# Splitting the gated activations before they are transposed, and transposing them by transfers from SyncE, in the expert stage of an early-fusion mixture-of-experts kernel

## The chip, the cores and the metric

The kernel runs on one core of one Trainium2 chip. The metric is the device time of one execution in microseconds. Five engines work side by side, each through its own instruction list in the order in which the program gives it: TensorE (PE in the profile, its weight loads PEld), VectorE (DVE), ScalarE (ACT), GpSimd (POOL) and SyncE (SP, which here only issues transfers). They meet at semaphores. Transfers run on 16 DMA engines that all queues share.

## The reference

```python
h = tokens(x)                             # 64 images -> 36 patches each, projected to 256, plus a class token
h = concatenate([h, txt], axis=1)         # 69 tokens x 64 = 4416 tokens of 256 values
h = h + attention(layernorm(h))
y = layernorm(h)
logits = y @ router                       # 8 experts, top 2 for each token
w13_out = ragged_dot(x_sort, moe_w13, group_sizes)      # 256 -> 1024, each expert its own weights
gate, up = split(w13_out, [512], axis=-1)
hidden = silu(gate) * up
out_dispatch = ragged_dot(hidden, moe_w2, group_sizes)  # 512 -> 256
h = h + zeros.at[token_ids_sort].add(out_dispatch * w_sort)
```

All is fp32. The change touches only what stands between `hidden` and `out_dispatch`, and the order around it.

## The kernel before

The program has two parts. `front()` does the patches, the attention, the router and the sorting of tokens to experts, and leaves three things: the normalised tokens with their weights for the experts in DRAM (`xn_rows`, 264 floats a row), the list `token_of` that says which 128 tokens make up each of 76 tiles, and `expert_of`, the expert of each tile. Some of the last tiles are padding, whose rows are all spare. It also fills `store_behind`, a number for each tile that says how far the scatters of the other parity must have come before its own scatter may go: for a tile whose expert differs from that of the tile before, and for every padding tile, it asks for the tile just before to have landed.

`experts()` then takes the 76 tiles one after the other (`N = TILES_MOE`). Each product is made of three fp16 products, since weights and activations are each split into a high and a low fp16 part (`terms`: hi by hi, hi by lo, lo by hi). For tile n:

- POOL gathers the tile's rows into `xg` (a piece of `wc`) by an indirect transfer; two buffers.
- PE transposes the 128x256 tile into bank 5 (two transposes by the identity); ACT copies it as fp16 to `x_hi`, DVE takes the difference as `x_lo`.
- PE makes the gate and the up product, 12 matmuls of 512 columns into `quad`; ACT takes the silu of the gate, DVE multiplies it with up into `hid`, fp32, 128 tokens by 512.
- PE transposes `hid` in four pieces of 128x128 into bank 4 (L1394); ACT copies that to `hid_hi` (L1307), DVE takes the difference as `hid_lo` (L1331).
- PE makes the second product, 12 matmuls of 256 columns, into bank 6 or 7 (L1424, through the helper at L1375); DVE scales it by the token's weight into `y` (L1354).
- POOL scatters `y` onto the output with addition, an indirect transfer (L1293). It waits for the scatter two tiles before, and for the one just before as far as `store_behind` asks.

The order on each engine is written out by hand in `step(t)`. On PE it is: transposes of hid(t-1), gate and up of t, transposes of x(t+1), second product of t-1. SP has nothing to do in this stage. Every intermediate has two buffers, chosen by the tile's parity. Below, step t starts with the first gate product of tile t.

## Time and profile before

| | |
|---|---|
| time, median of 3 runs | 825.34 us (822.24 to 830.76) |
| the profiled execution's own time | 829.55 us |
| its span in the trace | 827.4 us |
| mean granted clock of TensorE | 0.93 of full speed |
| expert stage in the trace, first transpose of a tile to the span's end | 462.3 to 827.4 us |
| busy share of the span: PE, DVE, POOL, ACT | 88%, 67%, 53%, 51% |
| DMA engines' mean busy share from 480 to 803 us | 0.38, at 60 GB/s |

The span is one profiled execution, times in it count from its start. A matmul's record is longer than the time until the next one starts, since matmuls are pipelined; the distance of starts is the rate. "issue" is time in which an engine waited for nothing that the profile shows. In rows of the kernel before, `bank<-idt,hid` is the transpose of the gated activations, `quad` the gate and up products, and `bank<-idt,wc` the transpose of a gathered tile.

### The profile page before, as it was taken

To read this page: it belongs to the slowest core of one execution; us is meant where nothing else is said; L and a number is where in the kernel's file an instruction comes from. 1 tells how busy PE (TensorE), PEld (TensorE's weight loads), DVE (VectorE), ACT (ScalarE), POOL (GpSimd) and SP (SyncE) were. 2 spreads that over 40 slices of the span, in tenths; PEclk is the share of its full clock that TensorE was granted. 3 is DMA by queue.
4 is the path that set the end of the run, shared out by engine and by line. 5 is a ranking of instruction groups with operands and counts; after the bars stand their busy time and mean duration, and the time that the engine had idled before them with its cause. 6 is when DMAs were issued, how large, how long until landed. Compare 5 with 4: busy or idle time off the path is not lost. (4 is left out here: it accounts for less than half of the span.)

```text
span 827.4 us, 27945 instructions
## 1 busy us (share of the span) xinstructions
PE 724.2 (88%) x9928; PEld 511.9 (62%) x9928; DVE 552.7 (67%) x1163; ACT 418.2 (51%) x951; POOL 435.6 (53%) x602
## 2 busy tenths in 40 slices
PE   6756989998999999989923599999999999999993
PEld 5634667776677776666722266666666666666662
DVE  6975888887888888787668455555555555555552
ACT  1233666677787777787637233333333333333330
POOL 5752554565766565553351255656555555555552
PEclk9985999999999999999655699999999999999997
DMA  8675576555454655454200034333333334343332
GB/s 286 210 240 177 152 244 190 152 163 153 138 163 147 174 159 153 125 169 123 82 25 7 27 54 66 54 64 57 62 59 60 60 59 65 55 66 54 64 55 24
DMA packets 64874, 91.81 MB, mean 111 GB/s; under 512 B 13176, under 2 KB 45704, under 8 KB 64679
## 3 DMA queue, kind: packets, MB, share of 16 engines
q1 hardware_dynamic: 49655, 66.81, 26.7%
q0 software_dynamic: 15088, 23.21, 16.8%
q8 instruction: 87, 1.43, 0.7%
q14 instruction: 44, 0.36, 0.1%
HBM read 58.95 MB, written 24.10 MB: 100 GB/s over the span
## 5 line engine op out<-in xcount | busy, mean ns | idle before, releaser
L1293 POOL DMA_INDIRECT out<-y,token_of x76 | 120.6, 1587 | 133.4 <-DVE own L1361 118.5
L1339 DVE SCALAR_TENSOR_TENSOR hid<-quad,up_scale,silu 128x512 f32<-128x512 f32 x76 | 57.0, 751 | 100.8 <-PE quad L1375 100.8
L1375 PE MATMUL quad<-w_hi,x_hi 128*128 x304 | 116.2, 382 | 1.2 <-DVE x_lo L1346 1.1
L1375 PE MATMUL quad<-w_lo,x_hi 128*128 x304 | 116.2, 382 | 0.0
L1375 PE MATMUL quad<-w_hi,x_lo 128*128 x304 | 116.2, 382 | 0.0
L652 DVE TENSOR_REDUCE nm_src<-quad 69x16 f32<-69x1104 f32 x64 | 83.0, 1297 | 35.4 <-PE quad L1055 35.2
L1307 ACT ACTIVATE hid_hi<-bank 128x512 f16<-128x512 f32 x76 | 45.4, 597 | 103.9 <-PE bank L1394 103.9
L919 ACT ACTIVATE probs<-quad 69x1104 f32<-69x1104 f32 x64 | 69.7, 1089 | 50.5 <-PE quad L1138 50.5
L1280 POOL DMA_INDIRECT wc<-xn_rows,token_of x74 | 73.4, 992 | 33.9 <-issue 21.9
L1375 PE MATMUL bank<-w_hi,hid_hi 128*128 x304 | 82.9, 273 | 1.6 <-ACT hid_hi L1307 1.6
L1375 PE MATMUL bank<-w_lo,hid_hi 128*128 x304 | 82.9, 273 | 0.0
L1375 PE MATMUL bank<-w_hi,hid_lo 128*128 x304 | 82.9, 273 | 0.0
L1313 ACT ACTIVATE silu<-quad,unscale 128x512 f32<-128x512 f32 x76 | 52.2, 687 | 54.8 <-PE quad L1375 54.8
L427 POOL TENSOR_SCALAR ve<-mv 128x1 f32<-128x1 f32 (+1 forms) x106 | 35.0, 330 | 63.8 <-DVE mv L715 35.6
L1331 DVE TENSOR_TENSOR hid_lo<-bank,hid_hi 128x512 f16<-128x512 f32 x76 | 52.6, 692 | 23.7 <-issue 19.1
L429 POOL TENSOR_TENSOR rs<-ve,eps_pow 128x1 f32<-128x1 f32 (+1 forms) x106 | 63.0, 595 | 8.8
L1319 ACT ACTIVATE x_hi<-bank 128x256 f16<-128x256 f32 x76 | 29.2, 384 | 74.2 <-PE bank L1415 74.2
L447 POOL TENSOR_TENSOR h<-hb,att 128x256 f32<-128x256 f32 (+1 forms) x35 | 34.4, 982 | 53.3 <-issue 27.2
L1354 DVE TENSOR_SCALAR y<-bank,weight 128x256 f32<-128x256 f32 x76 | 36.7, 483 | 35.3 <-PE bank L1375 35.3
L455 POOL TENSOR_TENSOR qk<-rot 128x256 f32<-128x256 f32 (+1 forms) x35 | 33.2, 949 | 48.1 <-DVE rot L697 47.9
L1134 PE MATMUL quad<-qT,kE 32*69 32x69 f32 x1024 | 45.9, 250 | 9.4 <-DVE nm_src L652 9.3
L1375 PEld LDWEIGHTS quad<-w_hi,x_lo 128*128 128x128 f16 x304 | 30.0, 99 | 36.2 <-issue 0.8
(230 smaller groups left out, 1866.0 us busy)
## 6 DMA issues: line engine op xcount, KB each, us to landing
w_lo<-in_experts_w SPq DMA_DIRECT2D x24, 512.0 KB, 5.9
w_raw<-in_experts_w SPq DMA_DIRECT2D x48, 256.0 KB, 4.9
xt<-in_patches SPq DMA_DIRECT2D x18, 384.0 KB, 5.7
h<-h_rows SPq DMA_DIRECT2D x34, 128.0 KB, 5.3
hb<-h_rows SPq DMA_DIRECT2D x34, 128.0 KB, 5.7
out<-h SPq DMA_DIRECT2D x34, 128.0 KB, 4.6
xn_rows<-xn SPq DMA_DIRECT2D x34, 128.0 KB, 4.6
vb<-v SPq DMA_DIRECT2D x30, 138.0 KB
```

Of the source, the lines that this page charges most:

```text
L429: nc.gpsimd.tensor_tensor(rs, ve, eps_pow[0:rs.shape[0], :], ALU.pow).then_inc(signal, 1)
L652: nc.vector.tensor_reduce(nm_src[b % 2][:, :].rearrange("p (g j) -> p g j", g=4)[:, :, 0:4], quad[0:SEQ, :, 0:4 * SEQ].rearrange("p g (j k ...
L919: nc.scalar.activation(probs[b % 2][:, :, :], quad[0:SEQ, :, 0:4 * SEQ], ACT.Exp, scale=HEAD_DIM ** -0.5).then_inc(s["probs_ready"], 1)
L1134: nc.tensor.matmul(quad[0:SEQ, g, j * SEQ:(j + 1) * SEQ], (kE, kO)[odd][band, c, at:at + SEQ], qT[band, c, at:at + SEQ], start=True, stop= ...
L1280: nc.gpsimd.indirect_dma_start(xg[q], None, xn_rows, bass.IndirectOffsetOnAxis(token_of[:, n:n + 1], 0)).then_inc(gathered[q], 16)
L1293: nc.gpsimd.indirect_dma_start(out, bass.IndirectOffsetOnAxis(token_of[:, n:n + 1], 0), y[q][:, :], None, compute_op=ALU.add).then_inc(add ...
L1307: nc.scalar.activation(hid_hi[q][:, :, :].rearrange("p c n -> p (c n)"), b4[:, :], ACT.Copy).then_inc(s["hid_hi_ready"], 1)
L1313: nc.scalar.activation(silu[q][:, :], quad[:, 2 * q, :], ACT.Silu, scale=unscale[:, 1:2]).then_inc(s["silu_ready"], 1)
L1331: nc.vector.tensor_tensor(hid_lo[q][:, :, :].rearrange("p c n -> p (c n)"), b4[:, :], hid_hi[q][:, :, :].rearrange("p c n -> p (c n)"), AL ...
L1339: nc.vector.scalar_tensor_tensor(out=hid[q][:, :], in0=quad[:, 2 * q + 1, :], scalar=up_scale[:, :], in1=silu[q][:, :], op0=ALU.mult, op1= ...
L1354: nc.vector.tensor_scalar(y[q][:, :], (b6, b7)[q][:, 0:DIM], weight[q][:, :], None, ALU.mult).then_inc(s["y_ready"], 1)
L1375: last = nc.tensor.matmul(dst, x[:, k, :], w[:, bass.ds(col + k * (2 * width if width == HIDDEN else width), width)], start=(k == 0 and m ...
```

## The change

The gated activations are now split first and transposed afterwards. ACT writes the fp16 high part of `hid` into half 0 of `hid_parts` (128 tokens x 2 x 512), DVE the low part into half 1, both from SBUF. SyncE then transposes the whole 128x1024 fp16 tile, eight blocks of 128x128, by one transfer into `hidT`, of which there are two. The second product of tile n moves from step n+1 to step n+2, and the scaling and the scatter with it. The scale factors `weight` get four buffers, the gathers three (`DEPTH`), and the first three gathers are issued by the front part. SyncE waits for both halves, and from tile 2 on for the second product of tile n-2, which frees the buffer that it writes. ACT and DVE wait, before they overwrite a half of `hid_parts`, for the transfer of tile n-2.

```diff
+DEPTH = 3
-        gathered = [sem(f"gathered{i}") for i in range(2)]
+        gathered = [sem(f"gathered{i}") for i in range(DEPTH)]
...
                     def _(pool):
                         def step(t):
-                            n, q, half, on, has = part(t + 2)
-                            if on and has(-2):
-                                pool.wait_ge(s["x_turned"], n - 1)
+                            n, q, half, on, has = part(t + DEPTH)
+                            if on and has(-DEPTH):
+                                pool.wait_ge(s["x_turned"], n - DEPTH + 1)
...
-                            n, q, half, on, has = part(t - 1)
+                            n, q, half, on, has = part(t - 2)
...
+                    @block.sync
+                    def _(sp):
+                        for n in range(N):
+                            q, half = n % 2, n // 2
+                            sp.wait_ge(s["hid_hi_ready"], n + 1)
+                            sp.wait_ge(s["hid_lo_ready"], n + 1)
+                            if n >= 2:
+                                sp.wait_ge(s["y_mm"], n - 1)
+                            sp.dma_start_transpose(hidT[q][:, :, :], hid_parts[q][:, :, :].rearrange("p a n -> p (a n)")).then_inc(hid_turned[q], 16)
...
                     def _(act):
-                            n, q, half, on, has = part(t - 1)
-                            if on:
-                                act.wait_ge(s["hid_turned"], n + 1)
-                                nc.scalar.activation(hid_hi[q][:, :, :].rearrange("p c n -> p (c n)"), b4[:, :], ACT.Copy).then_inc(s["hid_hi_ready"], 1)
...
+                            n, q, half, on, has = part(t)
+                            if on:
+                                act.wait_ge(s["hid_ready"], n + 1)
+                                if has(-2):
+                                    act.wait_ge(hid_turned[q], 16 * half)
+                                nc.scalar.activation(hid_parts[q][:, 0, :], hid[q][:, :], ACT.Copy).then_inc(s["hid_hi_ready"], 1)
...
                     def _(dve):
-                                nc.vector.tensor_tensor(hid_lo[q][:, :, :].rearrange("p c n -> p (c n)"), b4[:, :],
-                                                        hid_hi[q][:, :, :].rearrange("p c n -> p (c n)"), ALU.subtract).then_inc(s["hid_lo_ready"], 1)
...
+                            n, q, half, on, has = part(t)
+                            if on:
+                                dve.wait_ge(s["hid_hi_ready"], n + 1)
+                                if has(-2):
+                                    dve.wait_ge(hid_turned[q], 16 * half)
+                                nc.vector.tensor_tensor(hid_parts[q][:, 1, :], hid[q][:, :], hid_parts[q][:, 0, :], ALU.subtract).then_inc(s["hid_lo_ready"], 1)
+                            n, q, half, on, has = part(t - 2)
...
                     def _(pe):
-                            n, q, half, on, has = part(t - 1)
-                            if on:
-                                pe.wait_ge(s["hid_ready"], n + 1)
-                                if has(-1):
-                                    pe.wait_ge(s["hid_lo_ready"], n)
-                                for k in range(KH):
-                                    last = nc.tensor.transpose(b4[:, k * P:(k + 1) * P], hid[q][:, k * P:(k + 1) * P], idt[:, :])
-                                last.then_inc(s["hid_turned"], 1)
...
-                            n, q, half, on, has = part(t - 1)
+                            n, q, half, on, has = part(t - 2)
                             if on:
-                                pe.wait_ge(s["hid_hi_ready"], n + 1)
-                                pe.wait_ge(s["hid_lo_ready"], n + 1)
+                                pe.wait_ge(hid_turned[q], 16 * (half + 1))
```

On TensorE, between the second product of one tile (bank 6) and the gate product of the next, the list of before reads:

```order
L1375 MATMUL bank6<-w_lo,hid_hi0 128x256
L1375 MATMUL bank6<-w_hi,hid_lo0 128x256
L1394 MATMUL bank4<-idt,hid1 128x128 x4
L1375 ISA
L1375 MATMUL quad<-w_hi,x_hi0 128x512
```

and the changed one, where `hidT` takes the place of `hid_hi` and `hid_lo`:

```order
L1387 MATMUL bank7<-w_lo,hidT1 128x256
L1387 MATMUL bank7<-w_hi,hidT1 128x256
L1387 ISA
L1387 MATMUL quad<-w_hi,x_hi0 128x512
```

The four transposes are gone and nothing else stands in their place. Ahead of the gate product of an even tile (`x_hi0`) stood the second product of an even tile, two tiles back (`hid_hi0`); now that of an odd one stands there, three tiles back (`hidT1`).

On VectorE, one step in the middle of the stage, with the semaphores that each instruction waits for; before:

```order
L1331 TENSOR_TENSOR hid_lo1<-bank4,hid_hi1 128x512 [waits d_y_mm,d_hid_hi_ready]
L1339 SCALAR_TENSOR_TENSOR hid0<-quad,up_scale,silu0 128x512 [waits d_hid_turned,d_silu_ready,d_up_mm]
L1346 TENSOR_TENSOR x_lo1<-bank5,x_hi1 128x256 [waits d_up_mm,d_x_hi_ready]
L1354 TENSOR_SCALAR y1<-bank7,weight1 128x256 [waits d_added1,d_weight_ready,d_y_mm]
L1361 TENSOR_TENSOR own<-wc,is_expert 128x8 [waits d_weight_ready,gathered1]
```

and after:

```order
L1345 SCALAR_TENSOR_TENSOR hid0<-quad,up_scale,silu0 128x512 [waits d_hid_hi_ready,d_hid_lo_ready,d_silu_ready,d_up_mm]
L1352 TENSOR_TENSOR x_lo1<-bank5,x_hi1 128x256 [waits d_up_mm,d_x_hi_ready]
L1359 TENSOR_TENSOR hid_parts0<-hid0,hid_parts0 128x512 [waits d_hid_turned0,d_hid_hi_ready]
L1366 TENSOR_SCALAR y0<-bank6,weight2 128x256 [waits d_added0,d_weight_ready,d_y_mm]
L1373 TENSOR_TENSOR own<-wc,is_expert 128x8 [waits d_weight_ready,gathered2]
```

The low part is now taken of the tile of the same step (`hid0`, written two rows above it), behind `x_lo` and ahead of `y`, and it waits for a transfer's semaphore; the order of `hid` and `x_lo` is as it was.

On SyncE the stage was empty; now its list holds 76 rows like this one:

```order
L1310 DMA_TRANSPOSE hidT1<-hid_parts1 128x8x128 [waits d_y_mm,d_hid_lo_ready,d_hid_hi_ready]
```

SyncE has no other transfer in this stage, so a wait of it holds back only the transposes behind it.

## Rows read from the trace of the kernel before

**Rows 1.** Stretches: length, busy of PE, PEld, DVE, ACT, POOL; PEclk, DMA share, GB/s.

```profile
462.00:470.00 8.00, 6.41 (x16) 2.47 (x16) 1.23 (x4) 2.50 (x4) 0.94 (x1) 0.51 0.07 19
480.06:803.00 322.94, 322.94 (x2128) 215.00 (x2126) 176.56 (x426) 118.48 (x213) 183.27 (x142) 1.00 0.38 60
```

**Rows 2.** The chain that ended last, 598 to 606 us: start, length, engine, line.

```profile
598.65 2.59 PE quad L1375 x12
601.46 1.31 PE bank L1375 x12
602.77 0.44 PE bank L1394 x4
603.21 2.59 PE quad L1375 x12
```

**Rows 3.** By line and shape, 500 to 800 us: busy us, mean ns

```profile
L1394 PE MATMUL bank<-idt,hid 128*128 128x128 f32 x264 | 39.6, 273 | 0.0
L1331 DVE TENSOR_TENSOR hid_lo<-bank,hid_hi 128x512 f16<-128x512 f32 x66 | 45.6, 692 | 20.0 <-issue 17.8 <-ACT hid_hi L1307 2.2
L1307 ACT ACTIVATE hid_hi<-bank 128x512 f16<-128x512 f32 x66 | 39.4, 597 | 89.9 <-PE bank L1394 89.9
```

**Rows 4.** Timeline, one step around 601 us: start, length, engine, line, operation, [idle].

```profile
601.28 0.75 DVE L1339 SCALAR_TENSOR_TENSOR hid<-quad,up_scale,silu 128x512 f32<-128x512 f32 x1 [1.27 <-PE quad L1375]
601.29 0.27 PE L1375 MATMUL bank<-w_hi,hid_hi 128*128 x1
601.95 0.41 DVE L1346 TENSOR_TENSOR x_lo<-bank,x_hi 128x256 f16<-128x256 f32 x1
602.61 0.60 PE L1394 MATMUL bank<-idt,hid 128*128 128x128 f32 x4
602.81 0.48 DVE L1354 TENSOR_SCALAR y<-bank,weight 128x256 f32<-128x256 f32 x1 [0.45 <-PE bank L1375]
603.04 0.38 PE L1375 MATMUL quad<-w_hi,x_hi 128*128 x1
603.57 1.59 POOL L1293 DMA_INDIRECT out<-y,token_of  x1 [1.67 <-DVE own L1361]
```

**Rows 5.** DMA queues and us to landing, whole span, then 500 to 800 us.

```profile
q1 hardware_dynamic: 49655, 66.81, 26.7%
w_raw<-in_experts_w SPq DMA_DIRECT2D x48, 256.0 KB, 4.9
...
q0 software_dynamic: 12672, 17.58, 37.5%
out<-y,token_of POOLq DMA_INDIRECT x67, 3.9
```

**Rows 6.** Timeline of the stage's start, from the last gathers of the front part.

```profile
457.67 0.97 POOL L535 DMA_INDIRECT wc<-xn_rows,token_of  x1 [0.30 <-issue]
...
462.29 0.68 PE L1415 MATMUL bank<-idt,wc 128*128 128x128 f32 x2 [9.64 <-PEq L292]
470.27 0.42 DVE L1346 TENSOR_TENSOR x_lo<-bank,x_hi 128x256 f16<-128x256 f32 x1
470.94 0.39 PE L1375 MATMUL quad<-w_hi,x_hi 128*128 x1
474.41 0.41 DVE L1346 TENSOR_TENSOR x_lo<-bank,x_hi 128x256 f16<-128x256 f32 x1
475.50 0.38 PE L1375 MATMUL quad<-w_hi,x_hi 128*128 x1
```

**Rows 7.** Timeline of the stage's end: last tile's gate product, three of the scatters.

```profile
803.99 1.59 POOL L1293 DMA_INDIRECT out<-y,token_of  x1 [1.67 <-DVE y L1354]
...
808.02 0.38 PE L1375 MATMUL quad<-w_hi,x_hi 128*128 x1
...
809.44 1.57 POOL L1293 DMA_INDIRECT out<-y,token_of  x1 [3.86 <-DMA out<-y,token_of]
...
818.40 1.55 POOL L1293 DMA_INDIRECT out<-y,token_of  x1 [2.90 <-DMA out<-y,token_of]
```

More of the change, by code:

```diff
@@ L533, in _ @@
                             pool.wait_ge(xn_stored[par], 16 * len(range(par, G, 2)))
-                        for n in range(2):
+                        for n in range(DEPTH):
                             nc.gpsimd.indirect_dma_start(xg[n], None, xn_rows, bass.IndirectOffsetOnAxis(token_of[:, n:n + 1], 0)).then_inc(gathered[n], 16)
@@ L1254, in experts @@
                 silu, hid, y = ring("silu", [P, HIDDEN]), ring("hid", [P, HIDDEN]), ring("y", [P, DIM])
-                hid_hi, hid_lo = ring("hid_hi", [P, KH, P], fp16), ring("hid_lo", [P, KH, P], fp16)
-                own, weight = tb("own", [P, EXPERTS]), ring("weight", [P, 1])
+                hid_parts, hidT = ring("hid_parts", [P, 2, HIDDEN], fp16), [tb(f"hidT{i}", [P, 2 * KH, P], fp16) for i in range(2)]
+                own, weight = tb("own", [P, EXPERTS]), [tb(f"weight{i}", [P, 1]) for i in range(4)]
                 names = """x_turned x_hi_ready x_lo_ready gate_mm up_mm silu_ready hid_ready
-                    hid_turned hid_hi_ready hid_lo_ready y_mm y_ready own_ready weight_ready""".split()
+                    hid_hi_ready hid_lo_ready y_mm y_ready own_ready weight_ready""".split()
                 s = {n: sem("d_" + n) for n in names}
+                hid_turned = [sem(f"d_hid_turned{i}") for i in range(2)]
                 added = [sem(f"d_added{i}") for i in range(2)]
@@ L1353, in step @@
                                     dve.wait_ge(added[q], 16 * half)
[L1354 removed]
+                                nc.vector.tensor_scalar(y[q][:, :], (b6, b7)[q][:, 0:DIM], weight[n % 4][:, :], None, ALU.mult).then_inc(s["y_ready"], 1)
                             n, q, half, on, has = part(t + 1)
                             if on:
[L1358 removed]
+                                dve.wait_ge(gathered[n % DEPTH], 16 * (n // DEPTH + 1))
                                 if has(-1):
                                     dve.wait_ge(s["weight_ready"], n)
[L1361 removed]
+                                nc.vector.tensor_tensor(own[:, :], xg[n % DEPTH][:, DIM:], is_expert[:, n, :],
                                                         ALU.mult).then_inc(s["own_ready"], 1)
                                 dve.wait_ge(s["own_ready"], n + 1)
[L1364 to L1367 removed]
+                                if has(-4):
+                                    dve.wait_ge(s["y_ready"], n - 3)
+                                nc.vector.tensor_reduce(weight[n % 4][:, :], own[:, :], AX.X, ALU.add).then_inc(s["weight_ready"], 1)
+                        steps(step, -1, N + 2)
                     @block.tensor
@@ L1410, in step @@
                             if on:
-                                pe.wait_ge(gathered[q], 16 * (half + 1))
+                                pe.wait_ge(gathered[n % DEPTH], 16 * (n // DEPTH + 1))
                                 if has(-1):
@@ L1414, in step @@
                                 for k in range(KD):
-                                    last = nc.tensor.transpose(b5[:, k * P:(k + 1) * P], xg[q][:, k * P:(k + 1) * P], idt[:, :])
+                                    last = nc.tensor.transpose(b5[:, k * P:(k + 1) * P], xg[n % DEPTH][:, k * P:(k + 1) * P], idt[:, :])
                                 last.then_inc(s["x_turned"], 1)
-                            n, q, half, on, has = part(t - 1)
+                            n, q, half, on, has = part(t - 2)
                             if on:
-                                pe.wait_ge(s["hid_hi_ready"], n + 1)
-                                pe.wait_ge(s["hid_lo_ready"], n + 1)
+                                pe.wait_ge(hid_turned[q], 16 * (half + 1))
                                 if has(-2):
                                     pe.wait_ge(s["y_ready"], n - 1)
-                                terms((b6, b7)[q][:, 0:DIM], hid_hi[q], hid_lo[q], KH, expert.pop(n) * W_EXPERT + KD * 2 * HIDDEN,
+                                terms((b6, b7)[q][:, 0:DIM], hidT[q][:, 0:KH, :], hidT[q][:, KH:, :], KH, expert.pop(n) * W_EXPERT + KD * 2 * HIDDEN,
                                       DIM).then_inc(s["y_mm"], 1)
-                        steps(step, -1, N + 1)
+                        steps(step, -1, N + 2)
         front()
```

28 lines of the change are left out of this document (8 added, 20 removed).

## The prediction, made before the changed kernel had run

> **What bounds the kernel now.** I read the stretches of the expert stage first. From 480 to 803 us TensorE is busy for 322.94 of 322.94 us at the granted clock 1.00, while ACT has 118.48, DVE 176.56, POOL 183.27 and the DMA engines a share of 0.38 [rows 1]. Then the chain that ended last: it runs through TensorE without a break and repeats, gate and up 2.59 us, second product 1.31, transposes of hid 0.44, with starts 603.21 - 598.65 = 4.56 us apart [rows 2]. With steps 2 and 75 from the two ends, the period is (808.02 - 475.50) / 73 = 4.555 us [rows 6, 7]. So in this stage every microsecond that TensorE has less to do comes off, until something else is late. The front part is untouched but for one more gather at its end.
>
> **The change part by part, in one step of the stage.** Count from the step's first gate product, which is 603.04 - 4.555 = 598.49 [rows 4].
>
> *The transposes of hid leave TensorE.* Four matmuls, 0.44 us a tile in the chain [rows 2]; the timeline has 603.04 - 602.61 = 0.43 for the same [rows 4]. Nothing is put in their place. A step becomes 4.555 - 0.44 = 4.115 us, if TensorE stays the bound.
>
> *The next gate product's input.* It needs x_lo of tile t+1, which ends at 601.95 + 0.41 = 602.36 and is set by the chain up product, hid on DVE (from 601.28), x_lo; the change leaves these two first on DVE. Now the gate product can start at 602.61 at the earliest, where the transposes start today [rows 4]. The cover left is 0.25 us, less some 0.07 for the semaphore: 0.18 us. It was 0.6. I cost it at nothing; if the cover is gone, each 0.1 us costs 73 x 0.1 = 7.3 us.
>
> *The split on ACT and DVE.* Both read `hid` in SBUF, which no row shows, so I take 0.60 and 0.69 us, the same copy and difference out of PSUM [rows 3]; below, x_lo took 0.41 for half the elements [rows 4], so 0.41 is a floor, and twice the row a ceiling. hid ends at +3.54 (602.03). hid_hi runs from +3.60 to +4.20, hid_lo to +4.95, that is 0.83 us into the next step. There DVE is free: its next work is y, whose product ends with the step, and hid at 4.115 + 2.79. y (0.48 long) starts about 0.85 into the step and not at 0.2, so the scatter behind it starts that much later; with own and weight DVE is done by about 1.7, 1.1 us before hid is due at 2.79. So nothing waits; at the ceiling, 1.3 us more, hid would be some 0.2 us late.
>
> *The transfer.* It starts at +4.95. The second product of its tile stands two steps on, at 2 x 4.115 + 2.80 = 11.03 (601.29 - 598.49 = 2.80 [rows 4]). So from the end of hid_lo to the landing it may take **6.1 us**, with the semaphore 6.0, and TensorE doesn't notice. SyncE's other wait, the product of two tiles before, ends at 4.115 and is no limit. No row shows a transposing transfer. The nearest is a plain one of the same 256 KB from the same queue: 4.9 us from issue to landing, in a first part where the engines carry more [rows 5]. I take 4.9, nearer to 6.0 than I like. From below, the scatter of 128 KB lands in 3.9 [rows 5]; from above, twice the 256 KB row, 9.8, if the transposing costs as much again.
>
> *The DMA engines.* Scatter and gather take 0.375 x 4.555 = 1.71 us of all 16 engines a tile [rows 5]. SyncE's queue moved 66.81 MB in 26.7% of 827.4 us, 302 GB/s, so 256 KB more take 0.87 us; at the rate of the scatter and gather queue, 17.58 MB in 37.5% of 300 us = 156 GB/s, 1.68 [rows 5]. Share 2.58 to 3.39 of 4.115: busy 63 to 82%, not a bound. It would become one at 4.115 - 1.71 = 2.4 us a transfer, 109 GB/s.
>
> The Trainium skill has two sayings here. Its page "DMA: Bandwidth & Descriptors", section "Latency and other measured facts", gives a transposing transfer 261 GB/s, by which our 256 KB would take an estimated 1.0 us of the engines: no loss. Its page "VectorE: DVE Perf Modes", section "The three transpose paths", gives 1309 ns for one 128x128 block, against 390 on TensorE; if eight blocks add up, that is an estimated 10.5 us, and the change would lose as in the slow rival below. No row of before can say which holds for eight blocks in one transfer.
>
> *Three gathers, four weights, the moved scatter.* A gather is asked for a step earlier relative to its use, and none is late today. The third one at the front's end follows the second (457.67, 0.97 long) on POOL and ends near 460, before TensorE begins at 462.29 [rows 6]: nothing. POOL's two transfers a step stay.
>
> *Start.* TensorE is at the low clock there (0.51, [rows 1]) and step 1 waits for x_lo, which ends at 470.69, not for the transposes: step 1 starts at 470.75 instead of 470.94. Step 1 has now no second product, so step 2 waits for x_lo of tile 2, 474.82 less 0.19, and starts near 474.7 instead of 475.50 [rows 6]: 0.8 us gained. Then 73 steps of 0.44: 32.1. Step 75 starts at 474.7 + 73 x 4.115 = 775.1 instead of 808.02: **32.9 us earlier**.
>
> *End.* The last scatters go one behind the other: 809.44 to 818.40 is two distances of 4.48 us, 803.99 to 809.44 is 5.45 [rows 7]. They are longer than the new step, and the first of them now starts later. It started at 803.99, 4.03 before step 75. Now y of that tile is made in step 74, so its scatter starts about 1.5 us after step 75 begins (0.8 of DVE's queue, and 0.76 from y to the scatter, 603.57 - 602.81 [rows 4]). The last one then starts at 1.5 + 5.45 + 8.96 = 15.9 after step 75; it was 818.40 - 808.02 = 10.4. That gives back **5.5 us**. The last tile's own path, split, transfer 4.9, product, y, comes to 4.95 + 4.9 + 1.31 + 0.6 + 0.8 = 12.6, and is covered.
>
> *Sum.* 829.55 - 32.9 + 5.5 = 802.1 us against the profiled execution's own time. That execution was 4.2 above the median of 825.34; 27.4 less than the median is **798 us**.
>
> **The rivals.**
>
> *The full gain is trimmed (x chain or DMA jitter).* For it: the cover of x_lo falls to 0.18 us, and every scatter, gather and transpose now meets on the engines. If a step is 0.13 to 0.2 us longer, 73 x that = 10 to 15, so 808 to 813. Slow first steps belong here too: at clock 0.5 a step's 12 products take twice 2.59, 2.6 us more each. Against it: the chain of before holds 4.555 over 73 steps with nothing jittering.
>
> *The transfer is late (slower than before).* If L is the time from hid_lo to landing, second product, gate, up, hid and split close a loop of three steps: 3 x step = L + 1.31 + 4.95 + 0.1; the two buffers close one of two: 2 x step = L + 1.31 + 0.1. Nothing is lost up to L = 6.0. All is lost, 4.555 a step, at L = 13.67 - 6.36 = **7.3**, from which this rival decides. At L = 9.8 the step is the larger of 5.39 and 5.6, and the time 825 + 73 x (5.6 - 4.555) + 5.5 = about 907. The same happens if the engines need over 2.85 us a transfer (92 GB/s). For it: neighbouring elements of a source row go to different partitions here, where the plain transfers copy whole rows, and it meets two other transfers. Against: it would need half again the landing time of a plain transfer of its size, or a third of its rate.
>
> *The transfer is a little late (no change).* L between 6.6 and 7.3 with the 5.5 of the end: steps of 4.32 to 4.55, 817 to 831.
>
> *The change does not do what it says* would be that TensorE doesn't get shorter: the transposes stand in the chain with their full 0.44 [rows 2] and in no engine's shadow, so I give that nothing.
>
> **How the numbers follow.** Full gain 0.60 (792 to 806: the sum with 3 us either way for the start and the end, and half a per cent of spread between runs); trimmed 0.15 (806 to 817); a little late 0.09 (817 to 833); late and slower 0.16 (833 to 910). The range must leave out at most 0.2: it holds the first two and about half of the third, 790 to 824. One per cent, about what a measurement of this kernel can tell, is 8.3 us: faster is below 817, full plus trimmed and a little of the third, 0.77; slower, above 833.6, 0.16; the rest 0.07.
>
> **What the changed profile would show.** The chain should run through TensorE with quad 2.59, bank 1.31 and no third term, steps 4.11 to 4.13 apart, the stage's share of PE busy near all of it. A wait of the second product for a transfer, and a landing time above 6.0, would show the slow rival; a wait of the gate product for x_lo, of 0.1 us or so, the trimmed one. The DMA share should be 0.6 to 0.8 and the last four scatters should be serial, the last near 15.9 us after the last gate product starts. The prediction is wrong if the transfer takes more than 7 us, if DVE or ACT get slower when they read SBUF beside the transfers, or if TensorE's clock falls.

## The result: 803.41 us against 827.02, and the profile after

The changed kernel took 803.41 us, median of 6 runs (790.39 to 805.92), the kernel before 827.02 in 6 runs of its own; the ratio is 0.961, 95% interval 0.955 to 0.967. In a second set of 6 runs, beside 23 of before, it was 800.26 against 826.89, ratio 0.966 (0.962 to 0.971). The first ratio leaves out four of the six runs (802.9 to 805.9) as disturbed, hence its distance from 803.41 / 827.02 = 0.971; the second leaves out none. The forecast, 798 on 825.34, is 0.967.

| | before | after | after, second profile |
|---|---|---|---|
| span, us | 827.4 | 788.5 | 797.9 |
| first of the front part's gathers starts | 455.6 | 444.2 | 452.9 |
| stage: from there to the span's end | 371.8 | 344.3 | 345.0 |
| a step, mean of 73 | 4.555 | 4.118 | 4.118 |
| hid of tile 75, from the stage's start | 355.2 | 323.6 | 323.7 |
| last scatter, from that hid | 7.59 | 11.94 | 12.25 |
| mean granted clock of TensorE | 0.93 | 0.93 | 0.93 |

From here on the stage is counted from the start of the first gather, since all that the change touches lies behind it. It is 27.5 us shorter in the first profile and 26.8 in the second. The other 11.4 us between the first two spans stand ahead of it, where nothing is changed (see the section on them below).

The chain of after, in order of time (start, length, engine, line); it answers to [rows 2]:

```profile
600.44 2.59 PE quad L1387 x12
603.03 0.22 PE bank L1418 x2
603.25 1.31 PE bank L1387 x12
604.56 2.59 PE quad L1387 x12
607.15 0.22 PE bank L1418 x2
607.37 1.31 PE bank L1387 x12
```

The term of 0.44 us is gone. Gate and up 2.59, transposes of x 0.22, second product 1.31, starts 4.12 apart.

One step of after in the timeline; it answers to [rows 4], with the step's start at 600.28:

```profile
600.28 0.38 PE L1387 MATMUL quad<-w_hi,x_hi 128*128 x1
...
600.40 0.69 DVE L1359 TENSOR_TENSOR hid_parts<-hid,hid_parts 128x512 f16<-128x512 f32 x1 [0.36 <-issue]
...
601.00 0.48 DVE L1366 TENSOR_SCALAR y<-bank,weight 128x256 f32<-128x256 f32 x1
...
602.22 1.59 POOL L1296 DMA_INDIRECT out<-y,token_of  x1 [1.68 <-DVE own L1373]
...
603.07 0.75 DVE L1345 SCALAR_TENSOR_TENSOR hid<-quad,up_scale,silu 128x512 f32<-128x512 f32 x1 [1.32 <-PE quad L1387]
603.09 0.27 PE L1387 MATMUL bank<-w_hi,hidT 128*128 x1
...
603.29 0.38 ACT L1326 ACTIVATE x_hi<-bank 128x256 f16<-128x256 f32 x1 [0.82 <-PE bank L1418]
...
603.74 0.41 DVE L1352 TENSOR_TENSOR x_lo<-bank,x_hi 128x256 f16<-128x256 f32 x1
...
603.85 0.63 ACT L1332 ACTIVATE hid_parts<-hid 128x512 f16<-128x512 f32 x1 [0.18 <-DVE hid L1345]
...
604.11 1.00 POOL L1282 DMA_INDIRECT wc<-xn_rows,token_of  x1 [0.30 <-issue]
...
604.40 0.38 PE L1387 MATMUL quad<-w_hi,x_hi 128*128 x1
...
604.52 0.69 DVE L1359 TENSOR_TENSOR hid_parts<-hid,hid_parts 128x512 f16<-128x512 f32 x1 [0.36 <-issue]
```

Up product, hid, x_lo run as before: x_lo ends at 604.15, the next gate product starts at 604.40. That leaves x_lo a cover of 0.25 us. The high half of `hid_parts` is written from 603.85 (0.63 us), the low half from 604.52 (0.69), 4.24 us after the step began and so at the start of the next one; y and own come behind it. The scatter starts 1.94 us into this step, at 602.22, the gather 3.83, at 604.11; in the next step they stand at 1.48 and 3.37.

DMA queues of after from 500 to 760 us (packets, MB, share of 16 engines), which answer to the last rows of [rows 5]:

```profile
q0 software_dynamic: 12096, 16.78, 40.1%
q1 hardware_dynamic: 67015, 16.65, 38.3%
```

q1, SyncE's queue, carries nothing but the transposing transfers there: 38.3% of 260 us over 63 transfers is 1.58 us of all 16 engines for 256 KB. That is 1.8 times the 0.87 us that the same bytes took on this queue by [rows 5], in packets of some 248 bytes each (16.65 MB in 67015) where those had some 1350. The 1.58 is a mean: taken transfer by transfer the packets' times add up to 1.40 us in the median, and the slower ones raise it. What SyncE itself waited for, 470 to 790 us (total us, times, longest):

```profile
SPq L1309 <- DVE hid_parts L1359: 194.2, 70, 2.8
```

It stands idle for the low half nearly every time, 2.8 us in a step of 4.12, so its queue is no limit.

The end of the stage, timeline of after; it answers to [rows 7]:

```profile
765.01 0.38 PE L1387 MATMUL quad<-w_hi,x_hi 128*128 x1
...
766.49 1.55 POOL L1296 DMA_INDIRECT out<-y,token_of  x1 [2.55 <-DVE y L1366]
...
769.25 0.69 DVE L1359 TENSOR_TENSOR hid_parts<-hid,hid_parts 128x512 f16<-128x512 f32 x1 [0.70 <-ACT hid_parts L1332]
...
771.02 1.55 POOL L1296 DMA_INDIRECT out<-y,token_of  x1 [2.98 <-DVE y L1366]
...
773.19 0.39 PE L1387 MATMUL bank<-w_hi,hidT 128*128 x1 [2.63 <-DMA hidT<-hid_parts]
...
775.42 1.55 POOL L1296 DMA_INDIRECT out<-y,token_of  x1 [2.84 <-DMA out<-y,token_of]
...
775.97 0.48 DVE L1366 TENSOR_SCALAR y<-bank,weight 128x256 f32<-128x256 f32 x1 [4.88 <-PE bank L1387]
779.74 1.55 POOL L1296 DMA_INDIRECT out<-y,token_of  x1 [2.77 <-DMA out<-y,token_of]
```

The last tile's second product waits 2.6 us for its transfer, from the end of the low half at 769.94 to 773.19 is 3.25, but its scatter starts only at 779.74, behind three others.

And its start: POOL's gathers of the front part and TensorE's first transposes, after (against [rows 6]):

```profile
444.19 1.73 POOL L536 DMA_INDIRECT wc<-xn_rows,token_of  x1 [14.96 <-DVE token_of L832]
...
447.50 0.94 POOL L536 DMA_INDIRECT wc<-xn_rows,token_of  x1 [0.30 <-issue]
...
452.04 0.68 PE L1418 MATMUL bank<-idt,wc 128*128 128x128 f32 x2 [10.85 <-PEq L293]
```

### The profile page after: what moved, and what is told of

Read it like the earlier page. It is cut to its first block and busy times, and to the rows that moved or that the text cites. A ratio compares the mean times of both kernels' runs of the same rounds, so it can differ in the third digit from the quotient of the medians.

```text
span 788.5 us, 27483 instructions
## 1 busy us (share of the span) xinstructions
PE 688.5 (87%) x9624; PEld 476.1 (60%) x9624; DVE 544.4 (69%) x1163; ACT 420.6 (53%) x951; POOL 437.0 (55%) x602
## 5 line engine op out<-in xcount | busy, mean ns | idle before, releaser
L1387 PE MATMUL bank<-w_hi,hidT 128*128 x608 | 113.2, 274 | 2.6 <-DMA hidT<-hid_parts 2.6
L1387 PE MATMUL bank<-w_lo,hidT 128*128 x304 | 83.5, 275 | 0.0
L1359 DVE TENSOR_TENSOR hid_parts<-hid,hid_parts 128x512 f16<-128x512 f32 x76 | 52.7, 693 | 28.0 <-issue 16.7
L1387 PEld LDWEIGHTS bank<-w_hi,hidT 128*128 128x128 f16 x608 | 59.9, 98 | 9.6 <-issue 3.2
L1332 ACT ACTIVATE hid_parts<-hid 128x512 f16<-128x512 f32 x76 | 47.9, 630 | 15.2 <-DVE hid L1345 15.2
L1387 PEld LDWEIGHTS quad<-w_hi,x_hi 128*128 128x128 f16 x304 | 29.8, 98 | 36.7 <-issue 5.1
L997 PE MATMUL bank<-idt,xn 128*128 128x128 f32 (+1 forms) x140 | 28.5, 297 | 24.8 <-ACT logits L856 9.3
L1004 PE MATMUL bank<-wqkv_hi,fx_hi 128*128 128x512 f16 (+2 forms) x140 | 48.9, 349 | 1.5 <-DVE z L791 1.1
```

The lines of the kernel that those rows point to most:

```text
L1004: to = nc.tensor.matmul(dst, x[g % 2][:, k, 0:r], w[:, k, cols], start=(k == 0 and m == 0), stop=(k == KD - 1 and m == 2))
L1332: nc.scalar.activation(hid_parts[q][:, 0, :], hid[q][:, :], ACT.Copy).then_inc(s["hid_hi_ready"], 1)
L1359: nc.vector.tensor_tensor(hid_parts[q][:, 1, :], hid[q][:, :], hid_parts[q][:, 0, :], ALU.subtract).then_inc(s["hid_lo_ready"], 1)
L1387: last = nc.tensor.matmul(dst, x[:, k, :], w[:, bass.ds(col + k * (2 * width if width == HIDDEN else width), width)], start=(k == 0 and m ...
```

## The experiments

Each variant is of the changed kernel. Stage, as above, and step (the mean distance of hid from tile 2 to 75) are from the profile of each.

| kernel | median us | ratio to before (95%) | stage us | step us |
|---|---|---|---|---|
| before, again (2 runs) | 829.56 | 1.002 (0.995 to 1.008) | 373.0 | 4.557 |
| changed, again | 800.26 | 0.966 (0.962 to 0.971) | 345.0 | 4.118 |
| second product one tile behind | 852.96 | 1.033 (1.028 to 1.038) | 396.8 | 4.869 |
| every transfer twice | 835.26 | 1.009 (1.005 to 1.013) | 377.7 | 4.557 |
| transposes also on TensorE | 832.36 | 1.004 (1.001 to 1.008) | 377.3 | 4.555 |
| half of each transfer | 798.56 | 0.964 (0.962 to 0.967) | 344.9 | 4.118 |
| two gathers | 809.09 | 0.977 (0.973 to 0.981) | 354.2 | 4.260 |
| x by transfer too | 798.53 | 0.963 (0.960 to 0.967) | 348.4 | 4.165 |
| scatters of padding tiles freed | 798.34 | 0.967 (0.963 to 0.970) | 340.2 | 4.118 |
| x by transfer, even tiles | 825.36 | 0.997 (0.992 to 1.001) | 369.3 | 4.463 |
| the same, scatters freed | 826.34 | 0.999 (0.995 to 1.003) | 364.8 | 4.462 |
| the same, four gathers | 799.71 | 0.967 (0.961 to 0.973) | 340.4 | 4.096 |

### The two kernels again

> The changed kernel once more, unaltered. In its first profile the expert stage (first transpose of a tile to the span's end) took 336.5 us where it took 365.1 before, 28.6 less; the front part ended 10.25 us earlier than in the profile of before, though the change adds only a gather there. Theory A: the front part varies from one execution to the next by up to some 12 us in either kernel and the change has no part in it; then this profile shows the stage at 336 to 337 us again, steps 4.118 us apart, and a front part anywhere between 452 and 466 us. Rival: the change makes the front shorter; then it ends near 452 again. Ratio to before 0.96 to 0.97 by A, 0.955 by the rival.

> The kernel before once more, unaltered. Its front part ended at 462.29 us in the first profile and the stage took 365.1. Theory A: the stage is 365 us again to 0.5, and the front part ends anywhere between 452 and 466 us, as in the profiles of the changed kernel and its variants (452.0, 455.9, 461.0, 462.9, 466.1). Rival: it ends near 462 again.

Counted as in these expectations, from the first transposes on, the stage came out at 336.9 and 366.3 us, and the front part ended at 461.0 and 465.1; steps are 4.118 and 4.557. So the stage repeats to 1.2 us or better and what lies ahead of it doesn't: over the fourteen profiles of this study the first gather started anywhere from 444.2 to 459.3 us. Theory A holds in kind, but the stage of before was expected at 365 us to 0.5 and came out 1.2 longer, 1.1 of it in the last scatters (8.66 us behind hid of tile 75 instead of 7.59). The rival, a shorter front through the change, falls in the form that it had: the front ended at 461.0, not near 452. Two profiles of before alone wouldn't exclude a small part of it; the times do, since in the second set the whole kernel gains 26.6 us (826.89 to 800.26), no more than the stage's 26.8 to 28.7 (from the first gather, by the two profiles of each).

### The transposes back on TensorE

```diff
+                            n, q, half, on, has = part(t - 1)
+                            if on:
+                                pe.wait_ge(s["hid_ready"], n + 1)
+                                for k in range(KH):
+                                    last = nc.tensor.transpose(b4[:, k * P:(k + 1) * P], hid[q][:, k * P:(k + 1) * P], idt[:, :])
+                                last.then_inc(s["also_turned"], 1)
...
+                                    dve.wait_ge(s["also_turned"], n - 1)
```

> The changed kernel with the four transposes of the gated activations put back on TensorE at their old place, into bank 4, where nobody reads them; the transfer stays. Theory A (the gain is TensorE's time alone): a step is 4.118 + 0.44 = 4.56 us again, and the kernel 32 us slower than the changed one, some 4 us slower than the kernel before, since the longer end stays. Rival: part of the gain comes from ACT and DVE no longer waiting for bank 4; then it stays faster than before by 1% or more.

The chain of this variant shows the four transposes back in it:

```profile
601.25 0.44 PE bank L1405 x4
...
605.80 0.44 PE bank L1405 x4
```

Steps of 4.555 us, the stage 377.3, which is 32.6 more than 344.7, the mean of the two profiles of after; expected 32. The median is 32.1 us over that of the changed kernel on the same chip. The transfers run beside it as in the changed kernel. So the whole gain is TensorE's 0.44 us a tile, and the rest of the change, split from SBUF, third gather, moved scatter, gives nothing by itself; it only lets that 0.44 out, at the price of 4 us at the end.

### The second product one tile behind

```diff
-                            n, q, half, on, has = part(t - 2)
+                            n, q, half, on, has = part(t - 1)
```

on PE, DVE and POOL.

> The changed kernel with the second product one tile behind again (and its scaling and scatter), still with the transposing transfer. Theory A: the transfer lands 3.25 us after the low part is done, as the last tile's did, so a step is bound by the loop hid, split, transfer, second product: hid_lo ends 0.83 us into the next step, landing at 4.1, where the product could have begun at 2.80; the wait is 1.3 us, less what of the loop is shared, and a step becomes (4.95 + 3.25 + 1.31 + 0.1) / 2 = 4.8 us. That is 0.7 x 73 = 50 us more than the changed kernel, slower than the kernel before by some 20 us. Rival: the landing of the last tile was short because nothing else ran; with L of 5 in the middle a step is 5.7 us and the kernel 115 us slower than the changed one. Rival 2: the wait is not on the path and moving the product was not needed: no difference.

Steps average 4.869 us (expected 4.8), 52 us more stage than the changed kernel (expected 50). A piece of the chain shows the loop:

```profile
600.42 1.48 PE bank L1387 x12
601.90 2.60 PE quad L1387 x12
...
604.53 0.76 DVE hid L1345
...
605.98 0.70 DVE hid_parts L1359
...
606.73 3.02 DMA hidT<-hid_parts
...
609.89 1.48 PE bank L1387 x12
```

After the second product come the next gate and up, hid, the split, then 3.02 us of transfer, and the second product of that tile, for which TensorE had stood idle 1.06 us. Over the whole stage it waited 56 times for a transfer, 50.3 us in all, nearly the whole of the 52. What this run shows of landings:

```profile
DMA to landing us min/median/max: 3.0/3.1/4.6
```

That is the L of the prediction, 3.1 us in the median, not 4.9. Rival 1 (L of 5 with other traffic) falls, and rival 2 (moving the product was not needed) too: with the transfer in the path, one tile of distance would have made the change 3% slower than before. The second tile of distance is what the change rests on.

### Twice and half the transfer

```diff
                             sp.dma_start_transpose(hidT[q][:, :, :], hid_parts[q][:, :, :].rearrange("p a n -> p (a n)")).then_inc(hid_turned[q], 16)
+                            sp.dma_start_transpose(again[q][:, :, :], hid_parts[q][:, :, :].rearrange("p a n -> p (a n)")).then_inc(hid_turned[q], 16)
-                                pe.wait_ge(hid_turned[q], 16 * (half + 1))
+                                pe.wait_ge(hid_turned[q], 32 * (half + 1))
```

The waits of ACT and VectorE on this semaphore ask for twice the count as well.

> The changed kernel with every transposing transfer issued twice, the second into a tile that nobody reads; each wait asks for both. From 500 to 760 us 63 transfers took 38.3% of 16 engines, 1.58 us of all engines each, scatters and gathers 40.1%, 1.65 us a step. Theory A (the engines' time counts): the need becomes 1.65 + 3.16 = 4.81 us a step, over 4.118, so a step takes 4.8 to 4.9 us and the kernel is 50 to 57 us slower than the changed one. Rival (what counts is the time from issue to landing, and engines have room): 3.25 becomes 4.8 to 5.5, still under the 6.0 us of cover, no difference.

```diff
-                            sp.dma_start_transpose(hidT[q][:, :, :], hid_parts[q][:, :, :].rearrange("p a n -> p (a n)")).then_inc(hid_turned[q], 16)
+                            sp.dma_start_transpose(hidT[q][:, 0:KH, :], hid_parts[q][:, 0, :]).then_inc(hid_turned[q], 16)
```

> The changed kernel with half of each transfer: only the high part (128x512) is transposed, the low part of the transposed tile stays zero, so the third product of each term adds nothing (that part of the computation is left out). Theory A: the transfer was wholly hidden, so steps stay at 4.118 us and the time within 3 us of the changed kernel's; the time to landing falls from 3.1 by less than half, to about 2.5, if most of it is fixed, or to 1.6 if it goes by size. Rival: traffic from the full transfer costs something outside the chain, in the scatters of the end above all; then the end shortens from 14.7 us by 1 us or more.

With half the transfer the time, the stage and the steps are those of the changed kernel (344.9, 4.118), as theory A had it: the transfer is wholly hidden, with room. Its rival, a shorter end, falls as well: the last scatter starts 12.2 us after hid of tile 75, as in the two profiles of after. The time to landing can be read only in the last tile, where TensorE waits: 779.61 to 782.22, 2.6 us from the low half's end, against 3.25 with the full transfer, so most of it is fixed.

Doubled, the steps average 4.557 us, 33 us more stage, where 4.8 to 4.9 and 50 to 57 were expected. Of its 75 distances from hid to hid most are 4.12, and others up to 7.86. Waits of TensorE and ACT for the second transfer, 500 to 800 us (total, times, longest), and the queues from 500 to 760:

```profile
PE bank L1389 <- DMA again<-hid_parts: 22.6, 21, 2.2
...
ACT hid_parts L1334 <- DMA again<-hid_parts: 12.7, 17, 1.8
```

```profile
q1 hardware_dynamic: 119738, 29.73, 75.7%
q0 software_dynamic: 10938, 15.18, 35.6%
```

The two shares add up to 111%. So a packet's time counts waiting too, and shares add to more than the engines have: 1.65 + 2 x 1.58 = 4.81 us overstates the need, which was at most 4.557. With the median of 1.40 us a transfer the same sum is an estimated 4.45, 2% under what was measured. Theory A is right in kind, the doubled traffic is over a limit, and 6% off in size. Which limit is not shown: both transfers of a pair come from SyncE's one queue, and no run put the second one on another, so the 16 engines and the queue are not told apart. One of the ten executions took 1167.64 us, at a granted clock of 0.55, and is not explained.

### Two gathers instead of three

```diff
-DEPTH = 3
+DEPTH = 2
```

> The changed kernel with two gathers in flight instead of three, all else as changed. Theory A: no gather is late, steps stay at 4.118 us, time within 3 us of the changed kernel's. Rival: with the transfers on the same engines a gather lands later than its use, 2.9 us into the step after its request, and TensorE waits for it in some steps; then the transposes of x show waits for the gather and the stage is 5 us or more longer.

Theory A was mine in the prediction as well, and it falls: steps average 4.260 us, the stage is 9.5 us longer and the median 9 over the changed kernel's. TensorE's weight loads waited for gathers 20 times from 480 to 760 us (total, times, longest), and one of them in the timeline:

```profile
PEld bank L1418 <- DMA wc<-xn_rows,token_of: 14.9, 20, 2.3
```

```profile
698.57 1.00 POOL L1282 DMA_INDIRECT wc<-xn_rows,token_of  x1 [0.30 <-issue]
...
703.71 0.44 PE L1418 MATMUL bank<-idt,wc 128*128 128x128 f32 x2 [1.85 <-DMA wc<-xn_rows,token_of]
```

The gather for these transposes starts at 698.57, and its rows are there only at 703.71, 5.1 us later; TensorE has waited for 1.85. The window, from a gather's start to the transposes of its tile, was 4.7 us in the kernel before in nearly every step, is 7.4 in the changed one, and 3.5 in the median here, 3.3 where nothing is late. With the second product a tile later the scatter starts later in the step, and on POOL the gather stands behind it: the change had itself made the window of two buffers too short, and the third buffer gives it back.

### Going on: x by transfer too

The x tile is split in SBUF and transposed by a transfer of 128x512, all tiles with four gathers; then even tiles only, with three gathers; then with four.

```diff
+                        def turn_x(n):
+                            q = n % 2
+                            sp.wait_ge(s["x_hi_ready"], n + 1)
+                            sp.wait_ge(s["x_lo_ready"], n + 1)
+                            if n >= 2:
+                                sp.wait_ge(s["up_mm"], n - 1)
+                            sp.dma_start_transpose(x_T[q][:, :, :], x_parts[q][:, :, :].rearrange("p a n -> p (a n)")).then_inc(x_turned[q], 16)
...
-                                for k in range(KD):
-                                    last = nc.tensor.transpose(b5[:, k * P:(k + 1) * P], xg[n % DEPTH][:, k * P:(k + 1) * P], idt[:, :])
```

> The changed kernel, going on: the gathered tile is split in SBUF first too, two tiles ahead, and transposed by a transfer of 128x512 fp16 from SyncE, so that TensorE makes no transpose in this stage; four gathers in flight. Theory A (a step is TensorE's time while the engines have room): the two transposes were 0.22 us of the chain, so a step becomes 4.118 - 0.22 = 3.90 us, 16 us less over 73 steps, 2 to 3 given back at the start, where the first tile now waits for a transfer: 13 to 14 us under the changed kernel. Doubling the transfers gave steps of 4.557 us on average with 2 x 256 KB; taking away half a transfer, 0.5 x 1.58, puts the engines' need here at 3.77, just under 3.90. Rival: the third kind of transfer makes them meet, single ones land late, and the steps average 4.0 to 4.2: no gain.

> The changed kernel with the x transposes of even tiles done by a transfer of 128x512 (split in SBUF two tiles ahead), those of odd tiles on TensorE as before; three gathers in flight. Doing it for all tiles gave steps of 3.90 us in the median but 4.165 on average. Theory A (the engines' need is what is left): from the three means 4.557 at two units of transfer and 4.165 at one and a half, a unit is 0.78 us and the need at one and a quarter 3.97; TensorE's step is 4.118 - 0.11 = 4.01, so steps average 4.01 to 4.05 and the kernel is 5 to 8 us under the changed one. Rival: transfers that meet cause stalls below saturation too; then steps average 4.1 or more and nothing is gained.

With all tiles the step is 3.90 us in the median, as worked out, and 4.165 on average, with single ones up to 7.4. The first hid comes 2.5 us later than in the changed kernel, but by tile 2 that is made up, and the stage comes to 348.4 through its late steps: the rival holds, a tie with the changed kernel. ACT's waits for gathered rows, 480 to 760 us:

```profile
ACT x_parts L1333 <- DMA wc<-xn_rows,token_of: 31.9, 18, 4.9
```

On even tiles alone with three gathers it was worse, 4.463, against 4.01 to 4.05 expected. The rival's number, 4.1 or more, holds, but not by the meeting of transfers that it names. The same wait there:

```profile
ACT x_parts L1336 <- DMA wc<-xn_rows,token_of: 73.8, 31, 3.5
```

It comes at nearly every even tile, though there are fewer transfers: the split two tiles ahead asked for rows whose gather had begun 3.4 us before (597.29 to 600.69). The expectation had left this window out.

### The end

Each padding tile gets 128 spare output rows of its own (`put_of`), 1 MB of them are zeroed early in the front part instead of 128 KB, and the term that made these tiles wait is gone.

```diff
+                        then(nc.vector.tensor_scalar(mark, places, total, 1.0, ALU.subtract, ALU.add))
+                        then(nc.vector.tensor_scalar(mark, mark, 0.0, float(SPARE), ALU.max, ALU.mult))
+                        then(nc.vector.tensor_tensor(mark, found, mark, ALU.add))
+                        then(nc.vector.tensor_copy(put_of, mark))
-                        then(nc.vector.tensor_tensor(found[:, 1:], found[:, 1:], mark[:, 1:], ALU.add))
...
-                                nc.gpsimd.indirect_dma_start(out, bass.IndirectOffsetOnAxis(token_of[:, n:n + 1], 0), y[q][:, :], None,
+                                nc.gpsimd.indirect_dma_start(out, bass.IndirectOffsetOnAxis(put_of[:, n:n + 1], 0), y[q][:, :], None,
```

> The changed kernel, with the last scatters freed: each padding tile scatters onto spare output rows of its own, so it need not wait for the scatter before it. Three more small operations on DVE at the front part's end. Theory A: the serial scatters set the end; today the last one starts 14.7 us after the last gate product starts, and y of the last tile is ready at 11.4, so it starts near 11.8 and the stage is 2.5 to 3 us shorter, less 0.5 us for DVE: about 0.3% on the time, at the edge of what is measured, but plain in the trace. Rival: the scatters take turns on the DMA engines anyway and the end stays at 14 to 15 us.

POOL's last scatters there:

```profile
778.96 1.57 POOL L1301 DMA_INDIRECT out<-y,wc  x1 [2.55 <-DMA out<-y,wc]
783.07 1.56 POOL L1301 DMA_INDIRECT out<-y,wc  x1 [2.54 <-DVE y L1371]
784.94 1.55 POOL L1301 DMA_INDIRECT out<-y,wc  x1 [0.30 <-issue]
787.91 1.55 POOL L1301 DMA_INDIRECT out<-y,wc  x1 [1.42 <-DVE y L1371]
```

The last but one starts 1.87 us after the one before, not 4.4, and the last one as soon as its y is ready, 7.65 us after hid of tile 75 instead of 11.9 to 12.3. The stage takes 340.2 us, 4.4 less; expected were 2.5 to 3. The serial scatters do set the end. On the whole time nothing can be told (0.967, 0.963 to 0.970), since the part ahead of the stage varies by more. Nor is it shown that the eightfold zeroing there is free: in this variant and in the one of even tiles with freed scatters and three gathers the first softmax of the attention starts at 71.3 us, in the other profiles between 67.3 and 69.3 (with four gathers, which zeroes as much, at 69.1).

> Both of the above in one kernel. Theory A: their gains add, 5 to 8 and 2 to 3 us, so 7 to 11 us under the changed kernel, a ratio to before of 0.953 to 0.958. Rival: neither holds and it ties with the changed kernel at 0.96 to 0.966.

> The version with x transposes by transfer on even tiles and freed last scatters, now with four gathers in flight instead of three (two pairs of semaphores merged to make room). With three, steps averaged 4.463 us: ACT waited for a gather before the split of nearly every even tile, asked for only 3.4 us earlier (597.29 to 600.69). Theory A (it was the gather's window and not the engines' load): with a step more of window, steps average 4.01 to 4.05 us, the stage takes 332.4 - 5 to 8 = 325 to 327 us, and the ratio to before is near 0.957. Rival (the load): steps stay at 4.1 or more, as with all x transposes by transfer (4.165), and the stage is 332 us or longer.

With three gathers the pair is a tie with the kernel before, as x on even tiles alone; theory A of both falls, and so does the rival of the second, a tie with the changed kernel. With four gathers the steps fall to 4.096, so most of the loss was the gather's window; ACT still waits for a gather 8 times, and the 4.01 to 4.05 wanted are not reached. So the rival of the last variant, the load, is not ruled out for the rest: the steps are all but its 4.1, and the stage is no shorter than with freed scatters alone, as it said. Hid of tile 75 comes 1.7 us earlier than with freed scatters alone (321.9 for 323.6), and the last scatter 1.7 us later behind it (9.31 for 7.65): at 340.4 us the stage gains nothing on 340.2. Its time, 799.71, ties with the changed kernel's. So by the stage the version with freed scatters is 4.4 us, half a per cent, better than the changed kernel, and in the time none clearly beats it.

## Why the prediction was right

*TensorE sets the step.* 4.118 us measured, 4.115 worked out. With the transposes put back it was 4.555 again.

*The next gate product's input.* Cover 0.25 us less the semaphore, as worked out; no wait for x_lo shows from 470 us on.

*The split.* 0.63 and 0.69 us where I took 0.60 and 0.69. Out of SBUF the difference costs the same as out of PSUM and the copy 5% more.

*The transfer.* L was 3.1 us where I took 4.9 out of bounds of 3.9 and 9.8. It lies under my lower bound. The nearest row was a load of 256 KB from DRAM in the busy front part, which was a poor neighbour. The 3.1 is from the variant one tile behind, with longer steps. In the changed kernel only the last tile's landing shows (3.25 us from the low half's end), but the packets of all 76 transfers do: the first starts 1.24 us after the low half is done, the last one has ended 2.67 us after it in the median and 4.6 at most. The last tile landed 0.6 later than its last packet, so the slowest is an estimated 5.2, under the 6.0 of cover. The way of counting a loop held with one tile of distance, where L = 3.1 to 3.25 gives 4.73 to 4.8 and 4.869 was measured; the formulas for two tiles were not put to a test. The slow rival needed 7.3. One bound of the little-late rival was added up wrongly: steps of 4.32 give 814 us by its own terms, not 817.

*The engines.* 1.58 us a transfer, inside 0.87 to 1.68 and at the end that the scatters' rate gave; the DMA share became 0.79 and 0.80 (480 to 760 us, the two profiles), inside 0.63 to 0.82. The limit of 2.4 us a transfer could not be checked as such, the doubled one (2 x 1.58 by its packets' time) went over it.

*The two sayings of the Trainium skill.* No transfer of one block alone was run. For eight blocks in one transfer the runs decide against adding up the 1309 ns of the Trainium skill's "VectorE: DVE Perf Modes", section "The three transpose paths", which would be an estimated 10.5 us: 3.1 from issue to landing. The 261 GB/s of the Trainium skill's "DMA: Bandwidth & Descriptors", section "Latency and other measured facts", which it gives for a non-contiguous middle dimension, an estimated 1.0 us, compares with 1.58 us of packets' time, 166 GB/s, beside scatters and gathers.

*End.* The last scatter started 14.73 us after tile 75's gate product, where it was 10.38: 4.35 us given back, not 5.5. The first scatter of the four came 1.48 us after that product, as said (1.5), but I copied the long first distance of before, 5.45, and it was 4.53.

*Start.* Here a step failed: "the third one at the front's end ... nothing". The third gather ended at 448.44 and TensorE began at 452.04, 3.6 us later; before, the second ended at 458.64 and TensorE began at 462.29, again 3.6 us later; with two gathers in the changed kernel it was 455.15 and 458.80, and in the second profile of after 457.19 and 461.00, 3.8. From DVE's last operation it was 1.5 us before and 2.6 after. So TensorE's start follows POOL's last gather, and the third gather costs its 1.3 us. From the first transposes on, step 2 began after 12.33 us instead of 13.21, 0.9 gained for 0.8.

*Gathers.* I wrote that none is late and costed the third buffer at nothing. With three none is late, so the sum was not hurt, but the reason was wrong: I had moved the scatter later in my count and not the gather behind it, and two buffers would have cost 9.5 us. That the change had a third one was luck as far as the prediction goes.

*Sum.* From the first gather, hid of tile 75 comes 31.6 us earlier (355.2 for 323.6), where 32.9 less the gather's 1.3 would have been it, and the end gives back 4.35: 27.2 us, and 27.5 by the stage's length. Worked out were 27.4, of which the start was 1.3 too good and the end 1.1 too bad: the steps were right by their mechanism, and that these two errors cancel is luck. The trimmed and the late rivals didn't come.

## Where the two profiles' other 11 us were

Two stretches of the kernel before, then the first of them of after (length, busy of PE, PEld, DVE, ACT, POOL, granted clock, DMA share, GB/s):

```profile
68.00:84.00 16.00, 11.13 (x181) 7.38 (x180) 9.24 (x15) 6.02 (x16) 3.03 (x7) 0.60 0.43 147
84.00:100.00 16.00, 14.72 (x391) 10.43 (x384) 13.79 (x23) 9.89 (x21) 8.43 (x17) 1.00 0.56 164
```

```profile
68.00:84.00 16.00, 15.13 (x310) 10.11 (x302) 12.99 (x20) 8.44 (x20) 4.34 (x10) 0.89 0.69 218
```

Between 68 and 84 us TensorE of before is at clock 0.60 and busy for 11.13 us, that of after at 0.89 and 15.13. In the same place before has this wait, of which the first profile of after has 1.4 us at most, and the second profile of after this one:

```profile
DVE st L711 <- DMA h<-h_rows: 7.3, 1, 7.3
DVE st L712 <- DMA h<-h_rows: 6.5, 1, 6.5
```

DVE of before waits 7.3 us for one load of `h`. The first ten of the 64 images of the attention took 59.3 us there and 63.3 in the second profile of before, 52.5 in the first profile of after and 61.0 in the second, and from 54.5 to 64.2 in the others. Of the five groups of ten and more behind them each varies by 4.2 us at most, and the second by 0.2. The first ten make 6.8 of the 11.4 us, the third group 2.4 more. Up to 135 us the longest wait of DVE for such a load was 1.4 us in the first profile of after and 2.2 in the variant one tile behind (52.5 and 54.5 us for the first ten), 4.2 with x by transfer (58.8), and 5.9 to 7.3 in the other eleven (58.5 to 64.2). So in most executions, of either kernel, an early stretch waits long for a load of `h` and runs late, in some not, and that moves the whole by up to 12 us: more than a third of the effect that was to be measured. The wait goes with the loss; that it causes all of it was not tried.

## What to carry to other kernels

Where one engine is busy for the whole of a stage, its own small repeated work is the gain, here to 0.01 us a step, if all that replaces it closes its loops with room: write down for each new wait its loop over two and three steps and the latency at which it decides, and buy distance (here a second tile) rather than speed. Ask of an instruction added ahead of a hand-over between two parts of a program whether its engine is the last to arrive. When something is moved back in the step, move everything behind it in the same engine's list in the count too; its window shrinks, and a buffer more may be what keeps the change at its price. Split the profile into stages before comparing two spans, since a part that the change doesn't touch may differ by more than the change gives.

## What the runs showed of the hardware that I had not expected

A transposing transfer of 256 KB within SBUF landed 3.1 us after its issue in the median (one tile behind), sooner than the repeated plain transfers of 128 to 512 KB to or from DRAM on the same queue in the changed kernel (4.3 to 6.0 in the medians of its two profiles), though by its packets' time it took 1.8 times as much of the engines per byte, 1.6 times by the median transfer. Half the size was only 0.65 us quicker. The queues' shares of packets' time added up to 111% in the doubled variant, so such a share counts waiting as well, and a sum near 100% is not the limit that it seems. The lateness there comes in single steps, up to 3.7 us longer, while the median step stayed at 4.12.
